# Attention row sums: one row tile in eight is summed by VectorE, and GpSimd normalises the finished rows

## The reference

```python
q, k, v = (xn @ W.T, split into heads, for W in (Wq, Wk, Wv))
attn = softmax(q @ k.T * 512 ** -0.5, axis=-1) + rel_bias
out = attn @ v                          # [8, 1024, 512]
s = (out - mean(out)) * rsqrt(var(out) + 1e-5) * gamma + beta
y = square(relu(xn @ W_fc.T)) @ W_proj.T
g = silu(average of five steps of a spiking neuron driven by y)
result = x + s * g
```

## Time and profile before

| | |
|---|---|
| median of three runs | 3557.69 us (3556.57 to 3561.59) |
| profiled execution, its own time | 3560.06 us |
| its span from first to last instruction | 3558.3 us |
| granted TensorE clock, mean | 0.992 |
| TensorE matmul busy | 3434.7 us (97%) |
| ScalarE busy | 2634.2 us (74%) |
| VectorE busy | 2509.3 us (71%) |
| GpSimd busy | 1660.0 us (47%) |

### The profile page before, as it was taken

The page is one execution under the profiler, slowest core; times in us unless marked ns, Lnnn a source line. Parts: engine busy times, 40 slices in busy tenths (PEclk is TensorE's granted clock), DMA queues, the critical chain, the costliest instruction groups (busy, mean ns, idle before and its releaser), DMA issues.

```text
span 3558.3 us, 55234 instructions
## 1 busy us (share of the span) xinstructions
PE 3434.7 (97%) x19964; PEld 1445.5 (41%) x19964; DVE 2509.3 (71%) x3954; ACT 2634.2 (74%) x3929; POOL 1660.0 (47%) x961
## 2 busy tenths in 40 slices
PE   7999999999999998899999999999999999999996
PEld 3444444444444444333433433433433433433432
DVE  6555555555555546777888888878888888788887
ACT  6333333333333334999999999999999999999996
POOL 0012222111111112776675675675675675666662
PEclk9999999999999999999999999999999999999998
DMA  5222322332222213231332232232332322322322
GB/s 183 58 80 79 104 79 82 103 98 95 78 79 80 80 63 101 76 98 43 100 110 78 78 108 78 81 105 78 90 97 78 98 88 80 99 86 81 98 69 75
DMA packets 238751, 312.35 MB, mean 88 GB/s; under 512 B 96624, under 2 KB 132208, under 8 KB 238480
## 3 DMA queue, kind: packets, MB, share of 16 engines
q1 hardware_dynamic: 238480, 308.82, 27.8%
HBM read 174.65 MB, written 76.61 MB: 71 GB/s over the span
## 4 chain that ended last, share of the span: by engine, by line
ACT 37%; issue 10%; PE 8%; DVE 5%; SPq 1%; DMA 0%; ACTq 0%; DVEq 0%
ACT recurrence_or_probs L1277 19%; ACT s_sb L1284 18%; DVE s_sb L1360 3%; PE misc L1148 2%; PE acc L1228 2%; PE s_ps L1208 2%; PE s_ps L1194 2%; DVE gate_or_tokens L1471 1%; DVE x_or_queries L1397 1%; SPq L207 0%; DMA xT<-xnT 0%; DVE outT L1380 0%; DVE gate_or_tokens L1474 0%; DVE recurrence_or_probs L138 0%; PE misc L1130 0%
## 5 line engine op out<-in xcount | busy, mean ns | idle before, releaser
L1360 DVE TENSOR_SCALAR_CACHE_REDUCE s_sb<-s_ps 128x1024 f32<-128x1024 f32 x1024 | 1243.6, 1220 | 366.1 <-PE s_ps L1194 337.4
L1553 POOL TENSOR_TENSOR recurrence_or_probs<-recurrence_or_probs,toep 128x512 f32<-128x512 f32 (+1 forms) x375 | 1287.7, 3451 | 401.5 <-ACT recurrence_or_probs L1277 401.5
L1284 ACT ACTIVATE s_sb<-s_sb,nmax 128x1024 f32<-128x1024 f32 x1024 | 1194.7, 1167 | 18.7 <-DVE s_sb L1360 18.7
L1277 ACT ACTIVATE recurrence_or_probs<-s_ps 128x1024 f32<-128x1024 f32 x1024 | 1059.7, 1036 | 7.9 <-PE s_ps L1208 7.5
L434 PE MATMUL ps_fc<-xnT_part,w_fc 128*128 128x512 f16 x3072 | 708.0, 380 | 9.5 <-DMA xnT_part<-x_or_queries 5.0
L449 PE MATMUL ps_y<-w_pr,hid_part 128*128 128x512 f16 x3072 | 704.5, 379 | 4.1 <-issue 2.6
L580 ACT ACTIVATE relu<-ps_fc 128x512 f32<-128x512 f32 x256 | 152.8, 597 | 644.2 <-PE ps_fc L434 644.1
L118 POOL TENSOR_TENSOR recurrence_or_probs<-gate_or_tokens,beta_row 128x512 f32<-128x512 f32 x60 | 90.3, 1505 | 1105.8 <-DVE gate_or_tokens L146 1102.3
L746 DVE TENSOR_TENSOR hid<-relu 128x512 f32<-128x512 f32 x256 | 213.1, 833 | 549.5 <-ACT relu L580 549.5
L1228 PE MATMUL acc<-recurrence_or_probs,val 128*32 128x512 f32 x4096 | 546.8, 606 | 2.3 <-DVE recurrence_or_probs L1458 1.5
L434 PEld LDWEIGHTS ps_fc<-xnT_part,w_fc 128*128 128x128 f16 x3072 | 301.2, 98 | 374.9 <-issue 9.4
(11 more groups left out here) (160 smaller groups left out, 2559.5 us busy)
## 6 DMA issues: line engine op xcount, KB each, us to landing
toep<-table_rows SPq DMA_DIRECT2D x32, 2048.0 KB, 8.2
x_or_queries<-x_or_queries SPq DMA_DIRECT2D x384, 64.0 KB, 2.0
x_or_queries<-in_x SPq DMA_DIRECT2D x16, 1024.0 KB, 10.3
xnT<-xnT_part SPq DMA_DIRECT2D x32, 512.0 KB, 8.5
x_or_gate<-in_x SPq DMA_DIRECT2D x16, 1024.0 KB, 9.5
gate<-gate_or_tokens SPq DMA_DIRECT2D x16, 1024.0 KB, 4.5
base<-x_or_gate SPq DMA_DIRECT2D x16, 1024.0 KB, 6.8
xT<-xnT SPq DMA_DIRECT2D x32, 512.0 KB, 9.7
```

The lines of the kernel that those rows point to most:

```text
L1277: nc.scalar.activation(prob[:, k % PROBS, 2 * second:2 * second + 2, :].rearrange("p j n -> p (j n)"), s_ps[:, item_buffer(pair_item(m)), ...
L1284: nc.scalar.activation(s_sb[:, i % 4, :], s_sb[:, i % 4, :], ACT.Exp, bias=nmax[:, par, j, st:st + 1], scale=-1.0, accum_out=den[:, par, j ...
L1360: nc.vector.tensor_scalar(s_sb[:, i % 4, :], s_ps[:, item_buffer(tile_item(n)), :], -1.0, None, ALU.mult, ALU.min, accum_out=nmax[:, par, ...
L1553: nc.gpsimd.tensor_tensor(tile, tile, toep[:, par, :, at:at + width], ALU.add).then_inc(biased, 1)
```

## The change

A row tile with i % 8 == 0 (four of a group's 32) is no longer summed by ScalarE's accumulator. Its exp_sum has no accumulator output, and VectorE sums the buffer with a tensor_reduce (`add_up`), which stands in VectorE's list three tiles behind its row_max, so right after row_max of half-steps 1, 9, 17 and 25. Row_max of the tile that takes the buffer next, and ln_sums, also wait for `added`.

In all slots but the last, the 54 row tiles of F 0 to 12 and the first two of F 13 are normalised by GpSimd (`finish`), in three instructions: subtract the mean and multiply with the inverse root, multiply with gate, add base; each waits by semaphore for the one before. They stand after add_bias of steps 9 and 11 (in step 11 also after `subtracted`). newton stays on VectorE and now stands at half-step 12 of the slots with hg 0 or 2, b > 0. VectorE's own finish_normalise remains in and after the last slot. SP's store_tile waits for the same semaphore, which GpSimd now raises.

```diff
+FINISHED = ({9: (0,), 11: (1,)}, {9: (2,), 11: (3,)})
+ADDED, ADDED_LAG = 8, 3
...
+            def tile_earlier(self, h):
+
+                n = self.g * 32 + h + AHEAD - ADDED_LAG
+                return (n // 32, n // 32 % 2, n % 32) if 0 <= n < NG * 32 else None
+
+        def summed_by_vector(i):
+
+            return i % ADDED == 0
...
+        BY_GPSIMD = (2 * NB - 3) * 4 + 2
...
                 if s.finish:
-                    for t in s.normalise.values():
+                    for t in 2 * s.step, 2 * s.step + 1:
                         store_tile(s.done, t)
...
                 act.wait_ge(max_done, n + 1)
-                nc.scalar.activation(s_sb[:, i % 4, :], s_sb[:, i % 4, :], ACT.Exp, bias=nmax[:, par, j, st:st + 1], scale=-1.0,
-                                     accum_out=den[:, par, j, st:st + 1]).then_inc(sum_done, 1)
+                if summed_by_vector(i):
+                    nc.scalar.activation(s_sb[:, i % 4, :], s_sb[:, i % 4, :], ACT.Exp, bias=nmax[:, par, j, st:st + 1],
+                                         scale=-1.0).then_inc(sum_done, 1)
+                else:
+                    nc.scalar.activation(s_sb[:, i % 4, :], s_sb[:, i % 4, :], ACT.Exp, bias=nmax[:, par, j, st:st + 1], scale=-1.0,
+                                         accum_out=den[:, par, j, st:st + 1]).then_inc(sum_done, 1)
...
                 act.wait_ge(sum_done, G * 32 + half * 16 + 16)
+                act.wait_ge(added, (G * 32 + half * 16 + 16) // ADDED)
...
                 wait(dve, sum_done, n - 3)
+                if n >= 4 and summed_by_vector((i - 4) % 32):
+                    dve.wait_ge(added, (n - 4) // ADDED + 1)
...
+            def add_up(G, par, i):
+                n = G * 32 + i
+                j, st = i % 16 // 4, i // 16 * 4 + i % 4
+                dve.wait_ge(sum_done, n + 1)
+                nc.vector.tensor_reduce(den[:, par, j, st:st + 1], s_sb[:, i % 4, :], AX, ALU.add).then_inc(added, 1)
...
-                dve.wait_ge(fin_centred, n + 1)
+                dve.wait_ge(fin_centred, n + 1 - BY_GPSIMD)
+                if n == BY_GPSIMD:
+                    dve.wait_ge(fin_norm, BY_GPSIMD)
...
                         row_max(tiles[0], tiles[1], tiles[2] + second)
+                    earlier = s.tile_earlier(h)
+                    if earlier and summed_by_vector(earlier[2]):
+                        add_up(*earlier)
                     take_misc(b, hg, s, h)
                     if s.finish and s.step == 0 and h in STATISTICS:
                         finish_statistics(s.done, STATISTICS[h])
-                    if s.finish and h in s.normalise:
+                    if s.finish and s.last and h in s.normalise:
                         finish_normalise(s.done, s.normalise[h])
+                    if s.finish and not s.last and s.step == 0 and h == 12:
+                        newton(s.done)
...
+            def finish(F, t):
+
+                half, n = F % 2, F * 4 + t
+                row = tok[:, F % 3 * 4 + t, :]
+                pool.wait_ge(fin_newton, F * 4 + 4)
+                pool.wait_ge(fin_loaded[n % 4], (n // 4 + 1) * 32)
+                nc.gpsimd.tensor_scalar(row, row, fmv[:, half, t, 0:1], frs[:, half, 6, t:t + 1],
+                                        ALU.subtract, ALU.mult).then_inc(fin_step, 1)
+                pool.wait_ge(fin_step, n * 2 + 1)
+                nc.gpsimd.tensor_tensor(row, row, gate_t[:, n % 4, :], ALU.mult).then_inc(fin_step, 1)
+                pool.wait_ge(fin_step, n * 2 + 2)
+                nc.gpsimd.tensor_tensor(row, row, base_t[:, n % 4, :], ALU.add).then_inc(fin_norm, 1)
+                pool.wait_ge(fin_norm, n + 1)
...
+                    if s.finish and not s.last:
+                        for t in FINISHED[s.step].get(k, ()):
+                            finish(s.done, t)
```

More of the change, by code:

```diff
@@ L884, in attention @@
         sum_done = sem("sum_done")
+        added = sem("added")
         ln_done = sem("ln_done")
@@ L905, in attention @@
         fin_centred = sem("fin_centred")
+        fin_step = sem("fin_step")
         fin_norm = sem("fin_norm")
```

## The result

The kernel after takes 3663.64 us, the median of four runs (3661.72 to 3665.44), beside 3558.59 us for the kernel before in the same comparison (3556.57 to 3561.59). The ratio is 1.0292, with a 95% interval of 1.0276 to 1.0308: slower by 105 us, where 108.7 were forecast. The profiled execution took 3665.44 us (span 3663.6, mean granted clock 0.979).

The account below looks back on a forecast made before the run. ScalarE was taken to set the pace of the 32 attention slots. The terms -11.5 - 6.3 + 88 + 35 + 2.5 + 1 gave +108.7 us on 3560.06: 3668.8, as a median 3666 us, range 3610 to 3715.

Parts of the forecast that it names:

- (d): newton at half-step 12 waits for GpSimd's adds; ScalarE stands still 6.3 us in each of 14 slots, 88 us more.
- The rival of one add: All four newton instructions get in after one GpSimd add: 26 us from the delay, 3567 us in all; chance 0.04.
- the first rival: newton at half-step 12 is not held up by GpSimd: 3541 us, faster than before; chance 0.07.
- (e): TensorE idles behind the newton stall and its clock falls: 2.5 us in each of 14 slots, 35 us more.
- (a): ScalarE drops 128 accumulator reads at 0.09 us each, 11.5 us less; 2.5 us of it lost in newton's slots.
- (b): VectorE takes 128 sums at half-steps 1, 9, 17 and 25: no cost, or 7 us if idle time failed.
- the third rival: The new sums at half-steps 9 and 17 are also held up by GpSimd's adds: about 3705 us; chance 0.06.
- The remark on L1433: Half-step 1: L1433 behind the sum ends with GpSimd's add anyway, so the next row_max starts some 0.2 us later.
- (c): Normalising leaves VectorE: ScalarE's waits in 14 slots go, 6.3 us less; GpSimd's rows, 3.8 us at most, cost nothing.
- (f): In the last slot VectorE is the bound and has one more sum: 1 us more.

Follow-up runs that it names:

- newton_19: The kernel after with newton back at half-step 19: 3545.47 us, ratio 0.9954 to the kernel before.
- newton_12_alone: The kernel before with only newton moved, to half-step 12: 3668.56 us, ratio 1.0298 to the kernel before.
- short_adds: The kernel after, newton at 12, with GpSimd's adds of steps 3 to 7 cut to 16 columns a head: 3546.59 us, ratio 0.9956.
- first_at_12: The kernel after with newton's first instruction at half-step 12, the other three at 19: 3561.37 us, ratio 1.0000 to the kernel before.
- sums_only: The kernel before with the change's sums on VectorE, normalising left on VectorE, newton at half-step 19: 3565.89 us, ratio 1.0015.
- normalise_only_19: The kernel after with newton at half-step 19 and all sums left on ScalarE: 3552.22 us, ratio 0.9973 to the kernel before.
- one_in_four_19: The kernel after with newton at half-step 19 and two row tiles in eight summed by VectorE: 3546.43 us, ratio 0.9957 to the kernel before.

## Why the prediction was right, point by point

**(d), newton: right in place, mechanism and size.** Forecast were two instructions that end with GpSimd's adds, two short ones in the pause behind them, and an exp_sum late by 6.3 us. The trace has 4.29 and 4.42 us, 0.17 and 0.16, and 6.16. newton_19, newton_12_alone and short_adds each show it from another side, and first_at_12 that it takes two adds. The rival of one add falls with it: the second instruction took as long as the first. The Trainium skill (SBUF — State Buffer, Who interferes with whom) has a lock for the whole instruction, whatever its size: by that rule, now shown here for four elements and two SBUF inputs, the first rival was out.

**(e), TensorE: right.** 2.5 us a slot against 2.3 to 2.5. TensorE worked at half clock from 2580.2 to 2585.3, 5.1 us of the 5.5 taken. Of (a), half was to be lost in these slots; all of it is gone: with sums and normalising moved they take 74.52 us, and in newton_12_alone, with neither, 74.15.

**(a), the accumulator read: right.** Behind an exp_sum without it, at 2582.25, ScalarE was held up by TensorE; later in the slot it was not, and the distance is 1.04 us, against 1.13 with the read the earlier trace rows:

```profile
2600.89 1.14 ACT L1300 ACTIVATE s_sb<-s_sb,nmax 128x1024 f32<-128x1024 f32 x1
2601.93 1.01 ACT L1292 ACTIVATE recurrence_or_probs<-s_ps 128x1024 f32<-128x1024 f32 x1
```

Odd slots became shorter by 0.37 us, four times 0.09. The group's mean of 218 ns a read would have given more than twice that.

**(b), the sums: cost nothing, under a condition that the forecast did not see.** They ran at 1215 ns, 1211 to 1217, beside a busy GpSimd too, so the third rival falls; that agrees with the Trainium skill (SBUF — State Buffer, the same section), by which a tensor_reduce never contends on trn2. The remark on L1433 held too: the sum ahead of it takes up the time in which it stood still before (mean 170 ns now, 788 before). But they are free only as long as the normalising is gone: sums_only shows that, and the two terms (a) and (c) are not independent as the sum had them. Ahead of slot 0 they cost up to 2 us, which stood in no term.

**(c), the normalising: sign right, price of a row wrong.** GpSimd's tensor_scalar took 2.08 us, where I took 1.27 as the upper bound from the add of the same shape. A row is 4.63 us of instructions instead of 3.8 at most. The gaps held that too, the second row's barely:

```profile
2602.23 2.08 POOL L1584 TENSOR_SCALAR gate_or_tokens<-gate_or_tokens,fmv,frs 128x512 f32<-128x512 f32 x1
...
2607.11 1.27 POOL L1602 TENSOR_TENSOR recurrence_or_probs<-recurrence_or_probs,toep 128x512 f32<-128x512 f32 x1
```

That add, idle for 3.55 us ahead of it before, now follows after 0.09 us; but the list of waits between 1560 and 3480 us has none of TensorE for GpSimd. The gain alone was 9.6 us, 6 to 13 by the interval, against 6.3; in the profiled execution 8 us of it are the 14 slots, 0.57 each where 0.45 were forecast, and 2.5 the last slot, which (c) did not have.

**(f), the last slot: wrong, +1 forecast, -2.5 measured.** The earlier trace rows showed the clock at 0.50 there through four stretches; the kernel after keeps full clock at the same place:

```profile
3612.00:3614.00 2.00, 2.00 (x20) 1.70 (x17) 0.00 (x0) 1.97 (x5) 1.24 (x5) 1.00 0.04 8
```

I used that row as a price of half clock and not as something that the change could move. The sum of (f) cost nothing: the last slot takes 66.4 us from exp_pair 0 to the end in the kernel after, in sums_only and in normalise_only_19, which has no sum moved, and 68.8 before. By exp_pair 10 of that slot, in the stretch of half clock, the kernel before is 4.3 us behind, of which it makes up 1.9. In their traces either of the two moves alone keeps the full clock there; newton_12_alone (0.50 from 3612 to 3620, 68.9 us) and one_in_four_19 do not. What decides it was not tried.

The errors are small beside the sum because one term holds 88 us of it (14 waits of 6.16 us are 86), and that term rested on rows with the same two conditions, a busy GpSimd and a small instruction (L1433) or two SBUF inputs (L746).

## What to carry to other kernels

Before a small instruction on VectorE with two SBUF inputs is moved, look at what GpSimd does at the new place: there its price is what is left of GpSimd's instruction, and as long as GpSimd's instructions follow without a gap, the next link of a dependent chain pays for another one (two links did here, the other two fell into a pause of GpSimd). Then compare the delay with the slack of what is queued behind: the first 4 us in each slot cost 16 us in all, the next 4 cost 104. Two moves onto and off one engine are to be costed together, since the room that one makes is what the other uses.

## What the runs showed of the hardware

- A tensor_tensor of 128x4 took 4.29 and 4.42 us beside GpSimd's adds of 4.50 us, and 0.16 us with GpSimd idle (newton_19, short_adds).
- GpSimd's tensor_scalar with two per-partition operands is slower than its tensor_tensor of the same 128x512 in float32: 2076 against 1274 to 1280 ns.
- VectorE's tensor_reduce of 128x1024 took 1211 to 1217 ns in all 128 places of the kernel after, GpSimd busy or not.
- TensorE ran at half clock for 5.1 us after 6.20 us without work, and at full clock after 1.01 us without.
